# A conditioned matrix product with a low-rank part: tile 1 of x loaded between blocks of W, tile 0 multiplied block by block

## The reference, cut to what matters

```python
# x: (64, 32, 512); W0 = L0 weights (16, 32, 32); W: (512, 512); A: (5, 512, 32); Bw: (512, 32)
x = x + einsum('bct,bcd->bdt', x, W0[cond])          # per sample a 32x32 mix of its rows
base  = einsum('bsi,oi->bso', x, W)                  # 512 -> 512
low   = einsum('bsi,bir->bsr', x, A[label])          # 512 -> 32, A chosen per sample
delta = einsum('bsr,or->bso', low, Bw) * 0.5
return x + base + delta
```

## Time and profile before

| | us |
|---|---|
| three runs | 87.75, 88.84, 88.98; median 88.84 |
| the profiled execution, whole | 87.47 |
| its span, first to last instruction | 85.6 |
| TensorE busy in the span | 73.9 (86%) |
| VectorE, ScalarE, GpSimd busy | 41.6, 35.0, 32.6 |
| mean granted clock of TensorE | 0.94 of full speed |

### The profile page before, as it was taken

The page is one execution under the profiler, slowest core; times in us unless marked ns, Lnnn a source line. Parts: engine busy times, 40 slices in busy tenths (PEclk is TensorE's granted clock), DMA queues, the critical chain, the costliest instruction groups (busy, mean ns, idle before and its releaser), DMA issues.

```text
span 85.6 us, 2427 instructions
## 1 busy us (share of the span) xinstructions
PE 73.9 (86%) x1000; PEld 59.1 (69%) x1000; DVE 41.6 (49%) x65; ACT 35.0 (41%) x83; POOL 32.6 (38%) x74
## 2 busy tenths in 40 slices
PE   5977899998332499999999999999999999999940
PEld 4745899985221478758888867688887678867930
DVE  3029439996000074979929839692620626033110
ACT  2354438695000002687535831436563553603200
POOL 4713787999777910007889000570000010000000
PEclk9999569999995558999999999999999999999999
DMA  1899999480792000090049952000892000099675
GB/s 30 288 322 225 196 172 154 114 189 7 201 247 81 8 8 0 20 231 6 15 95 199 254 155 63 4 8 8 183 250 65 0 8 0 4 197 241 173 183 190
DMA packets 11727, 10.25 MB, mean 120 GB/s; under 512 B 1092, under 2 KB 9028, under 8 KB 11716
## 3 DMA queue, kind: packets, MB, share of 16 engines
q1 hardware_dynamic: 11200, 9.83, 49.4%
q0 software_dynamic: 512, 0.26, 1.4%
q10 hardware_dynamic: 4, 0.00, 0.0%
HBM read 5.90 MB, written 4.19 MB: 118 GB/s over the span
## 4 chain that ended last, share of the span: by engine, by line
PE 77%; issue 8%; DMA 6%; DVE 2%; SPq 1%; POOL 1%; POOLq 0%
PE p_u L634 15%; PE p_u L635 15%; PE p_u L636 15%; PE p_low L614 8%; DMA w_sb<-in_L_cond_W 6%; PE p_y L645 5%; PE p_u L640 4%; PE p_fold L623 3%; PE p_y L634 3%; PE p_y L635 2%; PE p_y L636 2%; DVE xt_last L464 2%; PE p_y L677 1%; PE p_y L669 1%; POOL w_sb L279 1%
## 5 line engine op out<-in xcount | busy, mean ns | idle before, releaser
L634 PE MATMUL p_u<-m_hi,xt_hi 128*128 128x512 f32 (+1 forms) x64 | 23.9, 374 | 0.0
L635 PE MATMUL p_u<-m_lo,xt_hi 128*128 128x512 f32 (+1 forms) x64 | 23.1, 361 | 0.0
L636 PE MATMUL p_u<-m_hi,xt_lo 128*128 128x512 f32 (+1 forms) x64 | 23.1, 361 | 0.0
L283 POOL DMA_INDIRECT w_sel<-in_L_cond_weights,w_row x16 | 15.8, 986 | 4.5 <-issue 3.9
L634 PEld LDWEIGHTS p_u<-m_hi,xt_hi 128*128 128x128 f32 x64 | 12.5, 195 | 2.0 <-issue 0.4
L636 PEld LDWEIGHTS p_u<-m_hi,xt_lo 128*128 128x128 f32 x64 | 12.4, 194 | 1.8
L635 PEld LDWEIGHTS p_u<-m_lo,xt_hi 128*128 128x128 f32 x64 | 12.5, 196 | 1.6
L458 DVE STREAM_TRANSPOSE xt<-x_sb 128x512 f32<-128x512 f32 x12 | 12.9, 1099 | 0.1
L614 PE MATMUL p_low<-a_sel,xt 128*32 128x32 f32 x448 | 7.6, 204 | 5.8 <-issue 5.8
L299 POOL TENSOR_TENSOR mix<-w_sel,fold_id 128x128 f32<-128x128 f32 (+1 forms) x4 | 2.1, 532 | 27.1 <-PE p_y L645 27.1
L614 PEld LDWEIGHTS p_low<-a_sel,xt 128*32 128x32 f32 x448 | 6.1, 115 | 8.0 <-issue 7.7
(11 more groups left out here) (80 smaller groups left out, 82.2 us busy)
## 6 DMA issues: line engine op xcount, KB each, us to landing
x_sb<-in_x SPq DMA_DIRECT2D x24, 128.0 KB
out<-y_sb SPq DMA_DIRECT2D x12, 256.0 KB, 4.0
w_sb<-in_L_cond_W SPq DMA_DIRECT2D x4, 256.0 KB, 4.7
x_rows<-in_x SPq DMA_DIRECT2D x2, 256.0 KB, 4.6
x_rows<-in_x SPq DMA_DIRECT2D x1, 512.0 KB
out<-y_two SPq DMA_DIRECT2D x4, 128.0 KB, 3.0
a_sb<-in_L_cond_lora_A SPq DMA_DIRECT2D x1, 320.0 KB
w_sel<-in_L_cond_weights,w_row POOLq DMA_INDIRECT x16, 2.5
```

The source lines that it names most:

```text
L283: nc.gpsimd.indirect_dma_start(out=w0_sel[:, t, :], out_offset=None, in_=W0_rows, in_offset=bass.IndirectOffsetOnAxis(ap=w0_row[:, t:t + 1 ...
L634: mm(to, xt_hi[:, slot, c, rows], m_hi[:, c, cols], start=(c == 0 and half != 1), stop=False)
L635: mm(to, xt_hi[:, slot, c, rows], m_lo[:, c, cols], start=False, stop=False)
L636: mm(to, xt_lo[:, slot, c, rows], m_hi[:, c, cols], start=False, stop=False)
```

## The change

- SyncE issues the load of tile 1 of x after the second block of W, in front of the third.
- The diagonal of the second block is added on GpSimd. GpSimd reads the positions for the first four copies of A before this block and those of the other four behind it.
- TensorE transposes tile 1 right after the second block. Tile 0 is then multiplied by 128 columns at a time for the first two blocks, with the transposes of the third and fourth block in between. Then come the left half of tile 1, the right half of tile 0 (256 columns), the transposes of `Bw` and the right half of tile 1.
- `cond` is spread in `p_u[1]` instead of `p_fold`, so that tile 1's transposes need not wait for its copy.
- ScalarE and VectorE split tile 1 of x between the second and the third block of W.

```diff
-            for o in W_ORDER:
+            for o in W_ORDER[:2]:
                 sp.dma_start(w_sb[:, o], W[P * o:P * (o + 1), :]).then_inc(s_w_in[o], 16)
             sp.dma_start(x_rows[:, 1], x_tile[1]).then_inc(s_rows_in[1], 16)
+            for o in W_ORDER[2:]:
+                sp.dma_start(w_sb[:, o], W[P * o:P * (o + 1), :]).then_inc(s_w_in[o], 16)
...
             pool.wait_ge(s_a_at, 2)
-            ats = positions(0)
-            for o in W_ORDER[2:]:
+            def diag_w(o):
+
                 pool.wait_ge(s_w_in[o], 16)
                 w_diag = w_sb[:, o, P * o:P * (o + 1)]
-                nc.gpsimd.tensor_tensor(w_diag, w_diag, ident[:], ALU.add).then_inc(s_diag_right, 1)
+                nc.gpsimd.tensor_tensor(w_diag, w_diag, ident[:], ALU.add).then_inc(s_diag_pool, 1)
+
+            ats = positions(0, slice(0, BT))
+            diag_w(W_ORDER[1])
+            ats = ats + positions(0, slice(BT, HS))
+            diag_w(W_ORDER[2])
+            diag_w(W_ORDER[3])
...
             split_rows(0, p_low)
-            for k in range(OC):
-                split_m(k)
+            split_m(0)
+            split_m(1)
             split_rows(1, p_fold)
+            split_m(2)
+            split_m(3)
...
             diag_w(0)
-            diag_w(1)
             split_rows(0, p_low)
             split_m(0)
             dve.wait_ge(s_cond_all, 1)
-            nc.vector.tensor_copy(cond_all[:], p_fold[:, 0:B]).then_inc(s_cond_sb, 1)
+            nc.vector.tensor_copy(cond_all[:], p_u[1][:, 0:B]).then_inc(s_cond_sb, 1)
             split_m(1)
+            split_rows(1, p_fold)
             split_m(2)
             split_m(3)
-            split_rows(1, p_fold)
...
-            def main_tile(bank, slot, u, cols=slice(0, O), half=None, chunks=range(C)):
+            def main_tile(bank, slot, u, cols=slice(0, O), first=True, chunks=range(C)):
...
-                if half is not None:
-                    pe.wait_ge(s_mlo, 2 * half + 2)
...
             pe.wait_ge(s_ones, 1)
-            mm(p_fold[:, 0:B], ones_r[:], cond_r[:], start=True, stop=True).then_inc(s_cond_all, 1)
-            pe.wait_ge(s_diag, 2)
+            mm(p_u[1][:, 0:B], ones_r[:], cond_r[:], start=True, stop=True).then_inc(s_cond_all, 1)
+            pe.wait_ge(s_diag_pool, 1)
             transpose_w(1)
-            pe.wait_ge(s_diag_right, 1)
+            transpose_rows(1, p_fold)
+
+            block = [slice(P * o, P * (o + 1)) for o in W_ORDER]
+            pe.wait_ge(s_xlo, 1)
+            pe.wait_ge(s_mlo, 1)
+            main_tile(p_u[0], 0, 0, block[0])
+            pe.wait_ge(s_diag_pool, 2)
             transpose_w(2)
-            pe.wait_ge(s_diag_right, 2)
+            pe.wait_ge(s_mlo, 2)
+            main_tile(p_u[0], 0, 0, block[1], first=False, chunks=(0, 1))
+            pe.wait_ge(s_diag_pool, 3)
             transpose_w(3)
-
-            pe.wait_ge(s_xlo, 1)
-            main_tile(p_u[0], 0, 0, left, half=0, chunks=(0, 1))
+            main_tile(p_u[0], 0, 0, block[1], first=False, chunks=(2, 3))
+            pe.wait_ge(s_xlo, 2)
             pe.wait_ge(s_cond_sb, 1)
-            transpose_rows(1, p_fold)
-            main_tile(p_u[0], 0, 0, left, half=0, chunks=(2, 3))
-            main_tile(p_u[0], 0, 0, right, half=1)
-            pe.wait_ge(s_xlo, 2)
-            main_tile(p_u[1], 0, 1, left, half=0)
+            main_tile(p_u[1], 0, 1, left)
+            pe.wait_ge(s_mlo, 4)
+            main_tile(p_u[0], 0, 0, right, first=False)
             transpose_b(p_y[0])
-            main_tile(p_u[1], 0, 1, right, half=1)
+            main_tile(p_u[1], 0, 1, right, first=False)
```

More of the change, by code:

```diff
@@ L149, in conditioned_lora_kernel @@
         s_diag = sem("s_diag")
-        s_diag_right = sem("s_diag_right")
+        s_diag_pool = sem("s_diag_pool")
         s_bw_rep = sem("s_bw_rep")
@@ L255, in _, with positions @@
                                         base=-R * j, pattern=[[-1, R]], channel_multiplier=1).then_inc(s_pool, 1)
-            def positions(k):
+            def positions(k, part=slice(0, HS)):
                 first = QS * k
                 _, ats = nc.values_load_multi_w_load_instructions(
-                    a_at[0:1, first:first + HS], engines=(mybir.EngineType.Pool,), min_val=0,
+                    a_at[0:1, first + part.start:first + part.stop], engines=(mybir.EngineType.Pool,), min_val=0,
                     max_val=(NL - 1) * C * R,
@@ L625, in spread_low @@
                 last.then_inc(s_fold, 1)
-            def main_tile(bank, slot, u, cols=slice(0, O), half=None, chunks=range(C)):
+            def main_tile(bank, slot, u, cols=slice(0, O), first=True, chunks=range(C)):
                 to = bank[:, cols]
                 rows = slice(P * u, P * (u + 1))
-                if half is not None:
-                    pe.wait_ge(s_mlo, 2 * half + 2)
                 for c in chunks:
-                    mm(to, xt_hi[:, slot, c, rows], m_hi[:, c, cols], start=(c == 0 and half != 1), stop=False)
+                    mm(to, xt_hi[:, slot, c, rows], m_hi[:, c, cols], start=(c == 0 and first), stop=False)
                     mm(to, xt_hi[:, slot, c, rows], m_lo[:, c, cols], start=False, stop=False)
```

## The result

| | before | after |
|---|---|---|
| runs, us | 87.75, 88.84, 88.98, 87.25 | 81.21, 81.58, 87.47, 86.58 |
| median, us | 88.3 | 84.08 |
| profiled execution, whole / span, us | 87.47 / 85.6 | 81.21 / 79.4 |
| mean granted clock | 0.94 | 0.979 |

The ratio after to before is **0.930** (95% interval 0.916 to 0.945). It is formed from the two runs at 81 us and, of the kernel before, the two at 87.25 and 87.75 us; the runs of 86.58 and 87.47 us, with a granted clock of 0.94, are left out of it, and they are why the median is 84.08. By the medians of all four runs the ratio is 0.952.

The account below looks back on a forecast made before the run. TensorE was taken as the bound, holding 77% of the chain of waits, with an 8 us hole. Moving the hole gave -5.0 us, half-clock work +1.0: 88.84 - 4.0 = 84.8 us, own range 82 to 86.

Parts of the forecast that it names:

- Part 1, loads: SyncE's load order: x of tile 1 lands at about 6.9 us; fourth diagonal and GpSimd's work behind it move 1.3 us later.
- full clock: TensorE with gaps filled may stay at 2.4 GHz, reaching low_group 0 at 19.0 us; possible gain about 1.5 us, not counted.
- Part 2: Diagonal of block 0 added on GpSimd, 0.45 us against 0.29 on VectorE: its transposes start 0.2 us later.
- Part 3: TensorE's new order: 1.0 us of idling saved, +1.2 us (0.0 to +4.1) for 24 matmuls of 128 columns at 0.11 us.
- rival D: Narrow matmuls take 0.23 us, TensorE reaches low_group 0 after gathers start: slower, 90.1 or 91.9 us; chance 0.20.
- Part 4, the hole: TensorE's 8 us near-standstill in low_group 0 beside six gathers: moves to low_group 1, which ends 5.0 us sooner.
- Case A: Hole belongs to the gathers: low_group 0 escapes, low_group 1 takes it, over at 31.9 us; 84.8 us; chance 0.38.
- term of 1.0 us for work at half clock: TensorE's work behind the hole was expected to run at half clock, adding 1.0 us.
- case B: Hole stays with low_group 0, starting at an instruction, not a gather: 87.6 to 89.0 us; chance 0.32.
- its own sign: Prediction is wrong if gathers run beside a dense group without a hole, or a hole stands where no gather is.

Follow-up runs that it names:

- late gathers: Kernel before plus one wait: GpSimd starts the six gathers only after low_group 1; 76.83 us, ratio 0.987, again 75.67 us, 0.983. Same wait on changed kernel: 76.50, 76.36 us.
- the long dense group: Kernel before with every product of low_group 0 issued four times, six gathers where they were: 98.33 and 93.83 us; kernel before 81.17 us.
- the run of four in a row without gathers: Kernel before with every product of low_group 0 issued four times and the six gathers started only after low_group 1: 93.25 and 93.02 us.

## Why the prediction was right, and where it was lucky

**Part 1, loads.** Right in order, 0.3 to 0.7 us too late in time: x of tile 1 landed at 6.6 us (6.9 expected), the third block by 7.55 us (8.2), the fourth diagonal came at 9.28 us for 9.6, the first gather at 11.45 for 11.8. One term was off: the 16 copies of A took 3.83 us instead of 4.79, so the six gathers came at 20.88 us and not at 22.1. The margin by which low_group 0 escaped was 0.6 us; the prediction had 1.6 us for the full clock and 0.2 us for an equal one.

**Part 2.** The second block's transposes began at 6.55 us instead of 6.62; +0.2 was expected.

**Part 3.** The step of 128-column matmuls is 0.11 us, as taken, and rival D is out. TensorE was at low_group 0 at 18.90 us (19.0 was given for the full clock, 20.5 without). But the gain there is the clock's and not the order's. Where the steps show 2.4 GHz throughout, the old order reached low_group 0 at 17.81 to 18.49 us in five profiles, and the new one at 18.60 to 18.90 us in four. Where they show 1.2 GHz for a time, the old order came at 19.66 to 20.66 us in three and the new one at 21.91 in one. So at equal clock the new order was later by some 0.7 us (medians 18.08 and 18.80 us), not by 0.2. That filling the gaps keeps the clock up is not borne out: the five profiles of the old order kept it with the gaps (2.07 us busy of 3.40 in the one shown above), and one of the new order lost it.

**Part 4, the hole.** Case A came out nearly to the letter: low_group 0 whole, low_group 1 from 24.62 us (24.6), held up inside the gathers. It ended at 30.7 us instead of 31.9, because the gathers ended 1.2 us sooner than reckoned. The term of 1.0 us for work at half clock behind the hole came to nothing: `mix_quad` took 1.90 us against 1.14 us at full clock, but from the end of low_group 1 to the end of the span both kernels took 48.7 us.

**The lucky part.** The forecast of 84.8 us met the median, 84.08 us, but that median mixes two groups. The two executions at 81 us are 3.4 us below the forecast. The profiled one shows why: of its 3.6 us, 1.2 us are the gathers' earlier end, 1.0 us the half-clock term, and 1.3 us lie between the two forecasts, 83.5 us for the profiled execution and 84.8 us for the median: that distance was taken over from the kernel before. That low_group 0 escaped at all was luck too: the gathers came at 20.88 us, and without the full clock, on which the prediction did not count, TensorE would by its own sum have been there from 20.5 to 21.9 us and so inside them. The two other executions, 87.47 and 86.58 us, look like that, case B's time. Their clock (0.937 and 0.940, against 0.979) fits, but they have no profile; this is argued, not shown.

**What the prediction did not see.** It took the hole for a fixed property of the kernel. It is not: in the five later comparisons 53 of 59 executions of the kernel before took 75.6 to 80 us (four more took 80.58 to 84.76 us, and two over 110), none the 87 to 89 us of the first, and in the two comparisons in which the changed kernel ran unchanged it gained nothing. So -7% (-5% by all runs) is the worth of the change only where the large hole is. By its own sign the prediction's view of the hole was wrong in part: gathers did run beside a dense group with hardly a hole, and pauses did stand where no gather is.

**What is shown of the cause.** All three profiles with the large hole have it beside the six gathers, with the same end, 1.2 to 1.3 us behind the last gather, whatever work was left. Beyond these, nine groups of 128 matmuls stood beside gathers, and none ran in 1.36 us: low_group 0 or 1 took 1.84 to 2.00 us in four profiles, and low_group 2 took 2.23 to 2.38 us in the five in which the added wait had moved gathers there (part of that can be instruction packets). Apart from one group that met only the end of the last gather (1.47 us), the 28 groups of 128 without gathers ran in 1.36 to 1.40 us, but for two with one pause of 0.3 us behind an instruction packet. Since moving the gathers moves the loss from one group to another, the small loss is the gathers'. The large hole is tied to them by its end, and by the one pair of profiles with four times the products, where the trickle is there with gathers and not with late ones. But no execution with late gathers was seen beside a kernel before that has the 8 us hole in every execution. **What turns a loss of 0.5 us into one of 8 us stays open.** The chip, what else ran on it, or the hour may have differed between the comparisons; within the one of the long dense group one execution shows the trickle; the other, 4.5 us shorter, has no profile.

## What to carry to other kernels

When a hole in a profile has no waiter, look at what stands beside it on every other engine, and at both of its ends; work that can be moved by a single wait (here six gathers, the last of them done 10 us before their mix matrices were built) is the cheapest test. As a change it was worth 0 to 2% here without the large hole, since it moves the smaller loss to low_group 2; what it is worth with the large hole was not measured. Before a gain is credited to a reordering, time both kernels again at another time and on another chip, and a kernel against itself, since two kernels that meet a disturbance at different places differ by the disturbance and not by their order.

## What was not expected of the hardware

- **A float32r matmul of 128 columns costs as much as one of 256**, at both clock levels: steps of 0.11 and 0.118 us at 2.4 GHz, 0.21 and 0.21 us at 1.2 GHz, and about the same duration (0.27 and 0.28 us). The prediction's reason, the weight load, is not shown by that. Cutting 12 matmuls of 256 columns into 24 of 128 nearly doubled their time (24 x 0.11 against 12 x 0.118 us). The 81 ns that the Trainium skill ("TensorE: Matmul & The Clock Gate", Back-to-back issue gap) gives for a pair with 128 columns is not reached here.
- **A dense stream of small matmuls outruns its instructions.** 128 matmuls with their weight loads take 1.4 us, and in the run of four in a row without gathers the next 256 instructions began only 3.5 to 4.9 us after the last ones, 1.35 to 1.57 us behind the end of their packet. The Trainium skill ("Runtime: NRT & Kernel Launch", Instruction fetch mechanics) has blocks of 256 instructions, as the pauses show, and calls the crossing mostly hidden. In these traces that holds for a single `low_group` (26 of 28 without gathers ran without a pause), and fails for four in a row.
- **A gather costs GpSimd 1.25 us** (0.94 us and a gap of 0.30), a plain transfer of the same size 0.55 us (3.28 / 6).
